# Block 0's start in another order: gates ahead of half the value's weights, one key weight tile on GpSimd, four constants behind the value's mixes, and block 1's statistics in two parts

## The chip, the cores and the metric

The kernel runs on one core of a Trainium2 chip. Its engines are TensorE (PE in the profile), VectorE (DVE), ScalarE (ACT), GpSimd (POOL) and SyncE (SP, which issues transfers). The metric is the device time of one execution in microseconds, the median of several; less is better.

## What is computed

One layer of an RWKV-like model over 2048 tokens of 512 features, in float32: a layer norm, an attention-like part with mixes of each token with its predecessor, a channel part, and a gated feed-forward part. Cut to what matters here, with `x` of the shape (1, 2048, 512):

```python
h = _layer_norm(x, ln1_g, ln1_b)
hh = _time_shift(h)
k = (h * tm_mk + hh * (1 - tm_mk)) @ Wk.T
v = (h * tm_mv + hh * (1 - tm_mv)) @ Wv.T
r = (h * tm_mr + hh * (1 - tm_mr)) @ Wr.T
wkv = _wkv_run(k, v, tm_first, tm_decay)   # elementwise: exponentials of k, and v
x = x + jax.nn.sigmoid(r) * wkv @ Wo.T
...                                          # channel part, then gated feed-forward part
```

## The kernel before

The tokens are cut into four blocks of 512. Activations lie with the features in the partitions, as four tiles of 128x512. A float32 product is made as three passes of TensorE: each operand is split into a high part (rounded, by a copy on ScalarE) and a low part (what the rounding left, by a subtraction on GpSimd or VectorE), and the passes are high x high, high x low and low x high (`three_passes`).

No scheduler orders the work. Each engine has its own program, written by hand, and the engines meet at counting semaphores. The order at the start of each program is what the change edits. For block 0 it goes so:

- The block's tokens are normed and transposed by TensorE into four PSUM banks. For each of r, k and v, ScalarE makes the previous token's share of a tile (`rest_of`, L746, into `made`), VectorE adds the token's own share (`mix`, L1123 and L1125; semaphore `op_made`), ScalarE makes the high part (`operand_hi`, L736; `op_hi`), and GpSimd the low part (`operand_lo`, L1459; `op_lo`). `made` is a ring of four tiles.
- Each weight matrix comes as four tiles. ScalarE makes the high parts (`matrix_hi`, L731; `w_hi`), and GpSimd (L1447) or VectorE (L1150, `matrix_lo`; for the last tile of Wr L1143) the low parts (`item_lo`).
- TensorE runs `receptance(0)` tile by tile as operands come (L517 to L521), then `key(0)` and `value(0)` bank by bank (`three_passes`, L485 to L487). A bank of `key(0)` is free when ScalarE's sigmoid has read the receptance from it (`receptance_gate`, L763; `r_gate`). A bank of `value(0)` is free when `wkv_weight` has read the key from it.
- `wkv_weight(0)` is shared by ScalarE (L770 into the bank, L773 into `e2`, L775 into the bank; it needs the constant `minus_bonus` and waits for `const_done` 7) and VectorE (L1160 for gate times `e2`, L1163 for bank times gate; `g_done`). `last_token` (twelve times L1107) saves the block's last token for the next block.
- In the middle of `value(0)` TensorE transposes block 1, which VectorE must have normed (`norm1(1)`) after its statistics (`norm1_stats(1)`: four bn_stats L1076, four bn_aggr L1079, L1050 and L1051) and after a power on GpSimd (`norm1(1)`, L1471).
- `later_constants` makes `minus_bonus` and the three constants of the channel part (L1041, L1035, L1036, L1038), each 128x4 or 128x8.

SyncE loads in one queue, in this order: block 0, the twelve tiles of Wr, Wk and Wv, block 1, Wo, and blocks 2 and 3. It isn't touched.

Of the kernel before, what the change touches and what calls it, by code (L numbers as in the profile page):

```python
# [30 lines left out]
KT = H // P  # L31
# [175 lines left out]
def build(nc, x, wts, wide, tall, vectors, identity, out):  # L207
# [3 lines left out]
    with ExitStack() as ctx:  # L211
# [117 lines left out]
        item_lo = [sem(f"item_lo{n}") for n in range(ITEMS // KT)]  # L329
        last_r_lo = sem("last_r_lo")  # L330
        const_done, table_loaded = sem("const_done"), sem("table_loaded")
# [150 lines left out]
        def _(pe):  # L482
# [18 lines left out]
            def features(kind, b, item, row, banks, done, bank_free, by_operand, halfway=None):  # L501
# [23 lines left out]
                else:  # L525
                    for j in range(KT):
                        if halfway is not None and j == KT // 2:
                            halfway()
                        bank_free(j)
                        for k in range(KT):  # L530
                            if j == 0:
                                if b == 0:
                                    pe.wait_ge(item_lo[item // KT], k + 1)
                                pe.wait_ge(op_lo, operand_at(kind, b) + k + 1)
                            mm = three_passes(banks[j][:], lambda p: weight(j, k, p),
                                              lambda p: place(kind, b, k, p), k == 0, k == KT - 1)
                        mm.then_inc(done, 1)
# [189 lines left out]
        def _(act):  # L727
# [249 lines left out]
            mixed("k", 0)  # L977
            matrix_hi(ITEM_V)
            receptance_gate(0)
            mixed("v", 0)  # L980
            act.wait_ge(const_done, 7)
# [45 lines left out]
        def _(dve):  # L1027
# [44 lines left out]

            def norm_stats(n, tile_of, stats, again=False):

                for s in range(SUBS):
                    dve.bn_stats(moments[:, s, :], tile_of(s)).then_inc(ln_moments, 1)  # L1076
                for s in range(SUBS):
                    dve.wait_ge(ln_moments, SUBS * n + s + 1)
                    dve.bn_aggr(stats[:, s, :], moments[:, s, :]).then_inc(ln_stats, 1)  # L1079
                dve.wait_ge(ln_stats, SUBS * (n + 1))  # L1080
                if again:
                    var_of_both(stats[:, :, 1], slice(None), ln_var)
                else:
                    dve.tensor_scalar(var_eps[:, 0], stats[:, :, 1], EPS, None, ALU.add).then_inc(ln_var, 1)

            def norm1_stats(b):
                dve.wait_ge(x_loaded[b - 1], 16)
                if b == BLOCKS - 1:
                    dve.wait_ge(ln_rstd, 3)
                norm_stats(nth_norm(1, b), lambda s: resid[:, b, s, :], stats1[:, b], again=True)  # L1090

# [286 lines left out]
            mix("r", 0)  # L1378
            later_constants()
            matrix_lo(ITEM_K, range(2))  # L1380
            mix("k", 0)
            matrix_lo(ITEM_K, range(2, KT))
            norm1_stats(1)
            mix("v", 0)
            last_token(0, 0)
            wkv_weight(0, range(2))
# [55 lines left out]
        def _(pool):  # L1442
            def matrix_lo(item, rows=range(KT)):
                for k in rows:
                    row = (item + k) % ROWS
                    pool.wait_ge(w_hi, item + k + 1)
                    pool.tensor_tensor(weights[:, row, 1, :], landing(item + k), weights[:, row, 0, :].bitcast(F32),  # L1447
                                       ALU.subtract).then_inc(item_lo[item // KT], 1)

            def x_added(b):  # L1450
# [84 lines left out]
            first_norm1()  # L1535
            pool.wait_ge(z1_ready, SUBS)
            matrix_lo(ITEM_R, range(KT - 1))
            operand_lo("r", 0)
            operand_lo("k", 0)
            matrix_lo(ITEM_V, range(3))  # L1540
            norm1(1)
            matrix_lo(ITEM_V, range(3, KT))
            operand_lo("v", 0)
            operand_lo("r", 1)
# [68 lines left out]
```

## Time and profile before

| | |
|---|---|
| time, median of 3 runs | 1074.23 us (1073.85 to 1074.23) |
| the profiled execution's own time | 1074.51 us |
| its span, first to last instruction | 1072.7 us |
| TensorE busy | 1057.1 us (99%), 4748 matmuls |
| VectorE, ScalarE, GpSimd busy | 632.5, 484.2 and 540.2 us |
| mean granted clock of TensorE | 0.998 |

Busy times are those of one profiled execution. Matmuls are pipelined, so a row's length is more than the distance to the next one: of two rows 0.227 us apart each is shown as 0.39 us. Instructions on the other engines overlap at their ends too. A line number is that of the kernel before, unless something else is said; in the changed kernel the lines stand 4 to 20 further down.

### The profile page before, as it was taken

The numbers are of one execution on the slowest core, as the hardware profiler recorded it, in microseconds if no ns is written. First come the engines' busy times: TensorE is split into PE (matmuls) and PEld (weight loads), VectorE is DVE, ScalarE is ACT, GpSimd is POOL, SyncE is SP. The second block draws the span as 40 slices with busy tenths as digits, with TensorE's granted clock in tenths as the row PEclk, the third lists the DMA queues.
The fourth block names the chain that finished last, engine by engine and source line by source line (L and its number), as shares of the span: only waits on it lengthen the run. The fifth ranks groups of instructions, "written<-read, shape, count | busy, mean of one in ns | idle before, by whom it ended". The sixth has DMA issues, their size and how long they took to land.

```text
span 1072.7 us, 13182 instructions
## 1 busy us (share of the span) xinstructions
PE 1057.1 (99%) x4748; PEld 873.8 (81%) x4748; DVE 632.5 (59%) x1104; ACT 484.2 (45%) x808; POOL 540.2 (50%) x453
## 2 busy tenths in 40 slices
PE   7999999999999999999999999999999999999998
PEld 6888888788888888888887888888887888888887
DVE  7888656786545545555459567676658333333334
ACT  6866676766444454333355433434354222222221
POOL 6686373735755545445345655555553333333322
PEclk9999999999999999999999999999999999999999
DMA  8002042267653345742412757564554464344422
GB/s 317 1 1 40 1 99 83 95 202 282 231 182 122 128 157 158 225 128 89 157 50 99 243 208 238 207 188 153 197 183 150 149 234 155 106 141 152 153 79 79
DMA packets 45234, 157.19 MB, mean 147 GB/s; under 512 B 4080, under 2 KB 4208, under 8 KB 40560
## 3 DMA queue, kind: packets, MB, share of 16 engines
q1 hardware_dynamic: 29712, 108.02, 28.8%
q0 software_dynamic: 15168, 48.24, 15.0%
q8 instruction: 38, 0.62, 0.2%
q14 instruction: 28, 0.23, 0.1%
q10 hardware_dynamic: 288, 0.09, 0.0%
HBM read 97.60 MB, written 58.72 MB: 146 GB/s over the span
## 4 chain that ended last, share of the span: by engine, by line
PE 87%; DVE 7%; POOL 2%; ACT 1%; DMA 1%; issue 1%; SPq 0%; ACTq 0%; DVEq 0%
PE bank L485 15%; PE bank L486 15%; PE bank L487 15%; PE bank L496 13%; PE bank L497 13%; PE bank L498 13%; DVE combo L1238 2%; DMA quart<-wide 1%; POOL operand L1459 1%; PE bank L555 1%; PE bank L653 1%; DVE resid L1264 1%; POOL weights L1447 0%; POOL weights L1459 0%; DVE raw L1245 0%
## 5 line engine op out<-in xcount | busy, mean ns | idle before, releaser
L1264 DVE TENSOR_TENSOR resid<-bank,resid 128x512 f32<-128x512 f32 x240 | 165.1, 690 | 239.8 <-PE bank L487 238.5
L1503 POOL TENSOR_TENSOR inner<-made,inner 128x512 fp32r<-128x512 f32 x128 | 166.8, 1326 | 200.5 <-ACT inner L871 200.5
L496 PE MATMUL bank<-combo,left 128*128 128x512 f32 x672 | 262.7, 391 | 4.7 <-DVE combo L1238 3.1
L498 PE MATMUL bank<-combo,left 128*128 128x512 f32 x672 | 261.5, 389 | 0.0
L497 PE MATMUL bank<-combo,left 128*128 128x512 f32 x672 | 261.5, 389 | 0.0
L485 PE MATMUL bank<-right,inner 128*128 128x512 f32 x512 | 199.2, 389 | 0.0
L486 PE MATMUL bank<-right,inner 128*128 128x512 f32 x512 | 199.2, 389 | 0.0
L487 PE MATMUL bank<-right,inner 128*128 128x512 f32 x512 | 199.2, 389 | 0.0
L1481 POOL TENSOR_TENSOR left<-quart,left 128x512 fp32r<-128x512 f32 x96 | 115.4, 1225 | 91.3 <-ACT left L839 46.8
L496 PEld LDWEIGHTS bank<-combo,left 128*128 128x128 f32 x672 | 126.1, 188 | 34.1 <-DVE combo L1238 4.0
L498 PEld LDWEIGHTS bank<-combo,left 128*128 128x128 f32 x672 | 126.1, 188 | 26.2
L497 PEld LDWEIGHTS bank<-combo,left 128*128 128x128 f32 x672 | 126.2, 188 | 25.7
L485 PEld LDWEIGHTS bank<-right,inner 128*128 128x128 f32 x512 | 96.1, 188 | 20.1
L487 PEld LDWEIGHTS bank<-right,inner 128*128 128x128 f32 x512 | 96.1, 188 | 20.0
L486 PEld LDWEIGHTS bank<-right,inner 128*128 128x128 f32 x512 | 96.1, 188 | 19.9
L1498 POOL TENSOR_TENSOR right<-tall_staged,right 128x512 fp32r<-128x512 f32 x62 | 80.8, 1312 | 59.2 <-ACT right L849 59.2
L892 ACT ACTIVATE made<-bank 128x512 f32<-128x512 f32 x64 | 38.1, 595 | 154.0 <-PE bank L498 154.0
L1459 POOL TENSOR_TENSOR operand<-made,operand 128x512 fp32r<-128x512 f32 x64 | 83.6, 1406 | 35.1 <-ACT operand L736 35.1
L1329 DVE TENSOR_TENSOR made<-bank,made 128x512 f32<-128x512 f32 x64 | 44.2, 691 | 60.4 <-ACT made L892 39.1
L871 ACT ACTIVATE inner<-made 128x512 fp32r<-128x512 f32 x128 | 77.2, 628 | 2.5 <-DVE made L1329 0.2
L880 ACT ACTIVATE made<-bank 128x512 f32<-128x512 f32 x64 | 37.6, 587 | 85.7 <-PE bank L498 85.7
L485 PE MATMUL bank<-operand,weights 128*128 128x512 f32 x176 | 69.5, 395 | 1.8 <-ACT held L763 1.8
(133 smaller groups left out, 1457.7 us busy)
## 6 DMA issues: line engine op xcount, KB each, us to landing
kept_left<-left SPq DMA_DIRECT2D x24, 1792.0 KB, 8.1
left<-kept_left POOLq DMA_DIRECT2D x24, 1024.0 KB, 6.9
left<-kept_left POOLq DMA_DIRECT2D x24, 768.0 KB, 5.0
tall_staged<-tall SPq DMA_DIRECT2D x64, 256.0 KB, 2.9
quart<-wide SPq DMA_DIRECT2D x24, 512.0 KB, 4.2
raw<-kept SPq DMA_DIRECT2D x32, 256.0 KB, 6.3
landed<-wts SPq DMA_DIRECT2D x20, 256.0 KB, 6.3
resid<-x POOLq DMA_DIRECT2D x4, 1024.0 KB, 9.2
```

Source lines behind the costliest of these rows:

```text
L485: pe.matmul(acc, left(0), right(0), start=first, stop=False)
L486: pe.matmul(acc, left(0), right(1), start=False, stop=False)
L487: return pe.matmul(acc, left(1), right(0), start=False, stop=last)
L496: pe.matmul(acc[:], hi, combo[:, c, k, 0, :], start=fresh and k == 0, stop=False, skip_group_check=True)
L497: pe.matmul(acc[:], hi, combo[:, c, k, 1, :], start=False, stop=False, skip_group_check=True)
L498: mm = pe.matmul(acc[:], lo, combo[:, c, k, 0, :], start=False, stop=k == 1, skip_group_check=True)
L871: act.activation(inner[:, h % 4, i, 0, :], made_at(n), ACT.Copy).then_inc(inner_hi, 1)
L1264: dve.tensor_tensor(tile, A[s][:], tile, ALU.add).then_inc(added, 1)
L1459: pool.tensor_tensor(place(kind, b, k, 1), made[:, (n + k) % RING, :], place(kind, b, k, 0).bitcast(F32), ALU.subtract).then_inc(op_lo, 1)
L1481: lo = pool.tensor_tensor(left[u % 2][:, 1, a[0]:a[0] + n, :], quart[:, a[0] + 1:a[0] + 1 + n, :], left[u % 2][:, 0, a[0]:a[0] + n, :].bit ...
L1498: pool.tensor_tensor(right[:, g % 2, i, 1, :], tall_staged[i][:], right[:, g % 2, i, 0, :].bitcast(F32), ALU.subtract).then_inc(right_lo, 1)
L1503: pool.tensor_tensor(inner[:, h % 4, i, 1, :], made_at(n), inner[:, h % 4, i, 0, :].bitcast(F32), ALU.subtract).then_inc(inner_lo, 1)
```

## The change

Five edits, all in block 0's start:

- On GpSimd, the first weight tile waits for `const_done` 3 in place of `z1_ready` 4. A new function `second_of_k_lo` makes the low part of Wk's tile 1 between the operands of r and of k, with a semaphore of its own, and TensorE's `key(0)` waits for that. Wv's fourth tile and the low operands of v now come ahead of `norm1(1)`.
- On ScalarE, `receptance_gate(0)` stands behind two of the four tiles of Wv in place of all four.
- On VectorE, `later_constants` is moved from ahead of k's mixes to behind v's mixes, and before k's mixes only tile 0 of Wk is left of two.
- On VectorE, `norm1_stats(1)` is cut in two: the four bn_stats stay ahead of v's mixes, and the rest stands behind the constants.

```diff
--- before.py
+++ after.py
@@ -327,7 +327,7 @@
         gate_kept = [sem(f"gate_kept{b}") for b in range(BLOCKS)]
         w_hi = sem("w_hi")
         item_lo = [sem(f"item_lo{n}") for n in range(ITEMS // KT)]
-        last_r_lo = sem("last_r_lo")
+        last_r_lo, second_k_lo = sem("last_r_lo"), sem("second_k_lo")
         const_done, table_loaded = sem("const_done"), sem("table_loaded")
         ln_moments, ln_stats, ln_var = sem("ln_moments"), sem("ln_stats"), sem("ln_var")
         ln_rstd, half_set = sem("ln_rstd"), sem("half_set")
@@ -529,8 +529,12 @@
                         bank_free(j)
                         for k in range(KT):
                             if j == 0:
-                                if b == 0:
+                                if b == 0 and kind != "k":
                                     pe.wait_ge(item_lo[item // KT], k + 1)
+                                elif b == 0 and k == 1:
+                                    pe.wait_ge(second_k_lo, 1)
+                                elif b == 0:
+                                    pe.wait_ge(item_lo[item // KT], max(k, 1))
                                 pe.wait_ge(op_lo, operand_at(kind, b) + k + 1)
                             mm = three_passes(banks[j][:], lambda p: weight(j, k, p),
                                               lambda p: place(kind, b, k, p), k == 0, k == KT - 1)
@@ -975,8 +979,9 @@
             mixed("r", 0, behind=1)
             matrix_hi(ITEM_K, range(1, KT))
             mixed("k", 0)
-            matrix_hi(ITEM_V)
+            matrix_hi(ITEM_V, range(2))
             receptance_gate(0)
+            matrix_hi(ITEM_V, range(2, KT))
             mixed("v", 0)
             act.wait_ge(const_done, 7)
             wkv_weight(0)
@@ -1070,10 +1075,14 @@
                     normed(s)
                 shares(slice(0, 3), 0)
 
-            def norm_stats(n, tile_of, stats, again=False):
-
+            def norm_moments(tile_of):
                 for s in range(SUBS):
                     dve.bn_stats(moments[:, s, :], tile_of(s)).then_inc(ln_moments, 1)
+
+            def norm_stats(n, tile_of, stats, again=False, moments_there=False):
+
+                if not moments_there:
+                    norm_moments(tile_of)
                 for s in range(SUBS):
                     dve.wait_ge(ln_moments, SUBS * n + s + 1)
                     dve.bn_aggr(stats[:, s, :], moments[:, s, :]).then_inc(ln_stats, 1)
@@ -1083,11 +1092,15 @@
                 else:
                     dve.tensor_scalar(var_eps[:, 0], stats[:, :, 1], EPS, None, ALU.add).then_inc(ln_var, 1)
 
-            def norm1_stats(b):
+            def norm1_moments(b):
+                dve.wait_ge(x_loaded[b - 1], 16)
+                norm_moments(lambda s: resid[:, b, s, :])
+
+            def norm1_stats(b, moments_there=False):
                 dve.wait_ge(x_loaded[b - 1], 16)
                 if b == BLOCKS - 1:
                     dve.wait_ge(ln_rstd, 3)
-                norm_stats(nth_norm(1, b), lambda s: resid[:, b, s, :], stats1[:, b], again=True)
+                norm_stats(nth_norm(1, b), lambda s: resid[:, b, s, :], stats1[:, b], True, moments_there)
 
             def norm1_tile(b, s):
                 dve.tensor_scalar(resid[:, b, s, :], resid[:, b, s, :], stats1[:, b, s, 0:1],
@@ -1376,12 +1389,13 @@
             last_of_r_lo()
             dve.wait_ge(const_done, 3)
             mix("r", 0)
-            later_constants()
-            matrix_lo(ITEM_K, range(2))
+            matrix_lo(ITEM_K, range(1))
             mix("k", 0)
             matrix_lo(ITEM_K, range(2, KT))
-            norm1_stats(1)
+            norm1_moments(1)
             mix("v", 0)
+            later_constants()
+            norm1_stats(1, moments_there=True)
             last_token(0, 0)
             wkv_weight(0, range(2))
             norm1(1)
@@ -1447,6 +1461,12 @@
                     pool.tensor_tensor(weights[:, row, 1, :], landing(item + k), weights[:, row, 0, :].bitcast(F32),
                                        ALU.subtract).then_inc(item_lo[item // KT], 1)
 
+            def second_of_k_lo():
+                row = ITEM_K + 1
+                pool.wait_ge(w_hi, row + 1)
+                pool.tensor_tensor(weights[:, row, 1, :], landing(row), weights[:, row, 0, :].bitcast(F32),
+                                   ALU.subtract).then_inc(second_k_lo, 1)
+
             def x_added(b):
 
                 pool.wait_ge(z2_ready, SUBS * (b + 1))
@@ -1533,14 +1553,14 @@
             pool.memset(minus_half[:], -0.5).then_inc(half_set, 1)
             pool.wait_ge(half_set, 1)
             first_norm1()
-            pool.wait_ge(z1_ready, SUBS)
+            pool.wait_ge(const_done, 3)
             matrix_lo(ITEM_R, range(KT - 1))
             operand_lo("r", 0)
+            second_of_k_lo()
             operand_lo("k", 0)
-            matrix_lo(ITEM_V, range(3))
+            matrix_lo(ITEM_V)
+            operand_lo("v", 0)
             norm1(1)
-            matrix_lo(ITEM_V, range(3, KT))
-            operand_lo("v", 0)
             operand_lo("r", 1)
             matrix_lo(ITEM_O)
             for b in range(1, BLOCKS):
```

VectorE, from the last mix of r to the first of k; before:

```order
L1125 SCALAR_TENSOR_TENSOR made<-bank,whole_g,whole_b 128x1
L1041 TENSOR_SCALAR minus_bonus<-vec 128x4
L1035 TENSOR_TENSOR whole_g<-vec 128x8
L1036 TENSOR_TENSOR whole_b<-vec 128x8
L1038 TENSOR_TENSOR rest_g<-vec,whole_g 128x8
L1150 TENSOR_TENSOR weights<-landed,weights 128x512 x2
L1123 SCALAR_TENSOR_TENSOR made<-bank,whole_g,made 128x511
L1125 SCALAR_TENSOR_TENSOR made<-bank,whole_g,whole_b 128x1
```

and now (L1136 and L1138 are the mixes, L1163 is the weight tile):

```order
L1138 SCALAR_TENSOR_TENSOR made<-bank,whole_g,whole_b 128x1
L1163 TENSOR_TENSOR weights<-landed,weights 128x512
L1136 SCALAR_TENSOR_TENSOR made<-bank,whole_g,made 128x511
L1138 SCALAR_TENSOR_TENSOR made<-bank,whole_g,whole_b 128x1
L1136 SCALAR_TENSOR_TENSOR made<-bank,whole_g,made 128x511
L1138 SCALAR_TENSOR_TENSOR made<-bank,whole_g,whole_b 128x1
L1136 SCALAR_TENSOR_TENSOR made<-bank,whole_g,made 128x511
L1138 SCALAR_TENSOR_TENSOR made<-bank,whole_g,whole_b 128x1
```

The four constants and one weight tile no longer stand between the mixes of r and those of k.

VectorE, from v's last mix to the first instruction of `wkv_weight` (L1160 of before, L1173 now); before:

```order
L1123 SCALAR_TENSOR_TENSOR made<-bank,whole_g,made 128x511
L1125 SCALAR_TENSOR_TENSOR made<-bank,whole_g,whole_b 128x1
L1107 SCALAR_TENSOR_TENSOR edge<-bank,rest_g,vec 128x1 x12
L1160 TENSOR_TENSOR held<-held,e_56 128x512
L1163 TENSOR_TENSOR held<-bank,held 128x512
```

and now:

```order
L1136 SCALAR_TENSOR_TENSOR made<-bank,whole_g,made 128x511
L1138 SCALAR_TENSOR_TENSOR made<-bank,whole_g,whole_b 128x1
L1046 TENSOR_SCALAR minus_bonus<-vec 128x4
L1040 TENSOR_TENSOR whole_g<-vec 128x8
L1041 TENSOR_TENSOR whole_b<-vec 128x8
L1043 TENSOR_TENSOR rest_g<-vec,whole_g 128x8
L1088 BN_AGGR stats<-moments 128x2 x4
L1055 TENSOR_SCALAR var_eps<-stats 128x4
L1056 TENSOR_SCALAR var_eps<-stats 128x4
L1120 SCALAR_TENSOR_TENSOR edge<-bank,rest_g,vec 128x1 x12
L1173 TENSOR_TENSOR held<-held,e_56 128x512
L1176 TENSOR_TENSOR held<-bank,held 128x512
```

The constants (L1046 to L1043) and the second half of block 1's statistics (L1088 to L1056) have come in ahead of `last_token` (L1120) and `wkv_weight`.

GpSimd, from the tiles of Wr to Wo; before (L1447 is a weight tile, L1459 a low operand, L1471 the power for block 1's norm):

```order
L1447 TENSOR_TENSOR weights<-landed,weights 128x512 x3
L1459 TENSOR_TENSOR operand<-made,operand 128x512 x8
L1447 TENSOR_TENSOR weights<-landed,weights 128x512 x3
L1471 TENSOR_TENSOR rstd<-var_eps,minus_half 128x8
L1447 TENSOR_TENSOR weights<-landed,weights 128x512
L1459 TENSOR_TENSOR operand<-made,operand 128x512 x8
L1447 TENSOR_TENSOR weights<-landed,weights 128x512 x4
```

and now (L1461 and L1467 are weight tiles, L1479 is a low operand, L1491 the power):

```order
L1461 TENSOR_TENSOR weights<-landed,weights 128x512 x3
L1479 TENSOR_TENSOR operand<-made,operand 128x512 x4
L1467 TENSOR_TENSOR weights<-landed,weights 128x512
L1479 TENSOR_TENSOR operand<-made,operand 128x512 x4
L1461 TENSOR_TENSOR weights<-landed,weights 128x512 x4
L1479 TENSOR_TENSOR operand<-made,operand 128x512 x4
L1491 TENSOR_TENSOR rstd<-var_eps,minus_half 128x8
L1479 TENSOR_TENSOR operand<-made,operand 128x512 x4
L1461 TENSOR_TENSOR weights<-landed,weights 128x512 x4
```

A weight tile now stands between the operands of r and of k, and the power stands behind the four operands of v.

## Rows read from the trace of the kernel before

**Rows 1.** The page: span, busy time and share of TensorE.

```profile
span 1072.7 us, 13182 instructions
...
PE 1057.1 (99%) x4748; PEld 873.8 (81%) x4748; DVE 632.5 (59%) x1104; ACT 484.2 (45%) x808; POOL 540.2 (50%) x453
```

**Rows 2.** Timeline of TensorE: start, length, instruction, idle time before it.

```profile
24.18 1.07 PE L521 MATMUL bank<-operand,weights 128*128 128x512 f32 x4
27.07 0.50 PE L485 MATMUL bank<-operand,weights 128*128 128x512 f32 x1 [1.82 <-ACT held L763]
...
28.43 0.63 PE L487 MATMUL bank<-operand,weights 128*128 128x512 f32 x1
...
39.68 0.39 PE L485 MATMUL bank<-operand,weights 128*128 128x512 f32 x1
```

**Rows 3.** Windows: stretch, length, busy time by engine, granted clock (PEclk), DMA share.

```profile
24.00:28.20 4.20, 2.38 (x11) 1.66 (x10) 4.20 (x5) 4.20 (x9) 4.20 (x4) 1.00 0.11 41
28.20:31.60 3.40, 3.40 (x10) 2.62 (x9) 3.37 (x11) 2.37 (x5) 3.40 (x3) 0.50 0.00 0
```

**Rows 4.** Timeline of ScalarE, columns as in rows 2.

```profile
17.31 1.66 ACT L731 ACTIVATE weights<-landed 128x512 fp32r<-128x512 f32 x3
...
21.48 0.63 ACT L736 ACTIVATE operand<-made 128x512 fp32r<-128x512 f32 x1 [0.51 <-DVE made L1125]
...
24.37 2.17 ACT L731 ACTIVATE weights<-landed 128x512 fp32r<-128x512 f32 x4
26.45 2.03 ACT L763 ACTIVATE held<-bank 128x512 f32<-128x512 f32 x4
...
34.41 0.64 ACT L770 ACTIVATE bank<-bank,minus_bonus 128x512 f32<-128x512 f32 x1
35.07 1.28 ACT L773 ACT_TABLE_LOAD   x1
36.37 0.60 ACT L773 ACTIVATE e<-bank 128x512 f32<-128x512 f32 x1
```

**Rows 5.** Timeline of VectorE.

```profile
17.01 1.26 DVE L1036 TENSOR_TENSOR whole_b<-vec 128x8 f32<-128x8 f32 x1
18.19 0.15 DVE L1038 TENSOR_TENSOR rest_g<-vec,whole_g 128x8 f32<-128x8 f32 x1
...
20.58 0.74 DVE L1123 SCALAR_TENSOR_TENSOR made<-bank,whole_g,made 128x511 f32<-128x511 f32 x1
...
23.72 3.25 DVE L1150 TENSOR_TENSOR weights<-landed,weights 128x512 fp32r<-128x512 f32 x2
26.89 2.46 DVE L1076 BATCH_NORM_STATS2 moments<-resid 128x6 f32<-128x512 f32 x4
...
29.66 0.97 DVE L1050 TENSOR_SCALAR var_eps<-stats 128x4 f32<-128x4 f32 x1
...
33.76 1.59 DVE L1107 SCALAR_TENSOR_TENSOR edge<-bank,rest_g,vec 128x1 f32<-128x1 f32 x12
...
37.79 0.69 DVE L1163 TENSOR_TENSOR held<-bank,held 128x512 f32<-128x512 f32 x1
```

**Rows 6.** Timeline of GpSimd.

```profile
14.44 5.07 POOL L1459 TENSOR_TENSOR operand<-made,operand 128x512 fp32r<-128x512 f32 x4
22.19 5.94 POOL L1459 TENSOR_TENSOR operand<-made,operand 128x512 fp32r<-128x512 f32 x4 [2.68 <-ACT operand L736]
28.09 3.77 POOL L1447 TENSOR_TENSOR weights<-landed,weights 128x512 fp32r<-128x512 f32 x3
31.81 1.64 POOL L1471 TENSOR_TENSOR rstd<-var_eps,minus_half 128x8 f32<-128x8 f32 x1
```

**Rows 7.** VectorE's L1051 after block 0 (durations in ns), and L1160 in block 0.

```profile
L1051 DVE TENSOR_SCALAR var_eps<-stats x3: 157/157/1332, 30.6 to 103.1; 128x4 f32<-128x4 f32 x3
...
L1160 DVE TENSOR_TENSOR held<-held,e x4: 685/693/1829, 37.1 to 44.7; 128x512 f32<-128x512 f32 x4
```

**Rows 8.** Timeline of TensorE near 827.

```profile
827.17 0.50 PE L496 MATMUL bank<-combo,left 128*128 128x512 f32 x1 [1.95 <-DVE combo L1238]
```


## The prediction, made before the changed kernel ran

> **What bounds the kernel now.** I first read the page: TensorE is busy for 1057.1 of 1072.7 us [rows 1]. Only its gaps and its slow stretches can be won, unless work is taken from it, and this change takes none. Then I read TensorE's timeline around the edited code [rows 2]. The receptance of block 0 ends with four matmuls from 24.18; the last starts near 24.86 and the next could start 0.23 later, at 25.1. The key of block 0 starts at 27.07, after an idle time of 1.82 us that the row puts down to ScalarE's sigmoid, `receptance_gate(0)`. From 28.4 at the latest the matmuls take 0.63 us apiece instead of 0.39. The windows say why: the granted clock is 1.00 up to 28.2 and 0.50 from 28.2 to 31.6 [rows 3], that is 1.2 GHz in place of 2.4. TensorE fell 1.1 us after it had started again, and 3.4 us at half speed cost 1.7 us. So the place has lost 1.8 + 1.7 = 3.5 us, 0.33% of the time. That is all a perfect edit could give here.
>
> Then I read ScalarE, VectorE and GpSimd over the same stretch [rows 4 to 6], to see what is late next.
>
> **The lock that sets the sizes.** Small VectorE operations sometimes take over a microsecond: the 128x8 product of L1036 takes 1.26 us and the one after it, L1038, only 0.15; L1050 takes 0.97 on 128x4 elements; two weight tiles of L1150 take 3.25 where L1160 does a tile of that size in 0.69 at best [rows 5, 7]. Each long one ends where a GpSimd tile ends (18.20, 30.6). Mixes, products from PSUM and bn_stats beside the same GpSimd tiles keep their length. So a VectorE operation that reads two SBUF tensors, or a tensor_scalar in SBUF, waits for the end of GpSimd's running tile and holds back the next one by some 0.45 us: four tiles of `operand_lo("k")` fill 22.19 to 28.09, or 5.9 us, against 3.72 us for three undisturbed (28.09 to 31.81, so 1.24 each) [rows 6]. After a wait of this kind a second small operation mostly slips through; one in three L1051 did not and took 1332 ns [rows 7].
>
> The Trainium skill (SBUF — State Buffer, "Who interferes with whom") has the same rule: whoever starts first holds the pair of ports that VectorE and GpSimd share for its whole instruction. By that rule the small operations are not free beside a busy GpSimd; without it the sum below would come out 2.2 us lower. The trace agrees, with the 1.26 and the 0.15 us.
>
> **The change, part by part.**
>
> *GpSimd's first wait.* `const_done` 3 comes three small products of VectorE, at most 0.15 us each [rows 5], after the last norm tile that it waited for. GpSimd's first tiles start up to 0.3 us later. What this moves is the low operands of r, which TensorE takes up in turn with its own work: I take nothing, and hold 0.3 us as the bound.
>
> *Constants away from the key, one key tile to GpSimd.* Between the mixes of r and of k, VectorE now does one tile in place of four constants and two tiles. It is ready for k's mixes near 17.9 instead of 20.58, but ScalarE's share of the first (L746) isn't done before 19.5 (three K tiles from 17.31, 0.52 each, and 0.76), so the mixes start about 19.6, 1.0 us sooner. ScalarE's first operand_hi of k still stands behind three L746 and comes at 20.8 instead of 21.48. ScalarE is free at 23.6 instead of 24.37 [rows 4]. GpSimd's added tile (1.24) lies in the pause that it had before 22.19, from 20.2 to 21.4, and the k tiles start at 21.45. With two of them held back by VectorE's tiles 2 and 3, as before, they end at 27.3.
>
> *Gates ahead of half the V tiles.* ScalarE does two V tiles (1.04) to 24.65, and the gates when the bank is done: receptance's first bank ends its row near 24.6, so the gate starts at 24.75 and ends at 25.3 (0.57) instead of 27.02. `key(0)` starts at 25.35, 1.7 us sooner. It wants its four low operands at 25.4, 26.1, 26.8 and 27.5; they come at 22.7, 24.0, 25.7 and 27.3. All fit, the last by 0.1 to 0.2 us. No gap worth a fall of the clock is left, so 48 matmuls at 0.227 us end at 36.35 instead of 39.68 [rows 2]. Up to here 3.3 us are won. The V tiles' loads stand ahead of block 1's in SP's in-order queue; no step here issues or moves a transfer.
>
> *What is late next: `value(0)`.* Its first bank waits for `g_done` 1 (L1163), which needs ScalarE's exponentials, and they need `const_done` 7. I follow GpSimd's tile ends, since VectorE's small operations now meet them. GpSimd is busy without a pause from 21.45: k to 27.3, V to 32.25 (4 x 1.24), v to 37.25 (tile ends 33.5, 34.75, 36.0), and only then `norm1(1)`, 1.60 long. VectorE: tile 3 of K ends near 26.2, bn_stats 2.4 more, mixes of v from 28.6 (0.79 each, the last held by ScalarE to 30.95), free at 31.75. There L1041 waits for 32.25 and L1036 for 33.5, so `const_done` 7 is at 33.65. Four bn_aggr (0.35) lead to L1050, which waits for 34.75; then the twelve L1107 (1.5) end at 36.35. ScalarE, free at 32.4, waits to 33.7; L770 0.66, table load 1.29, exp 0.60: e2 at 36.3 [rows 4]. L1160 thus arrives at 36.35, inside the tile that ends at 37.25, then takes 0.6, and L1163 0.69: `g_done` 1 at 38.6, against 37.79 + 0.69 = 38.48 before [rows 5]. The constants and the statistics have moved from before the key to before the value's gate, and that gate isn't sooner at all.
>
> So `value(0)` starts at 38.65 instead of 39.68: 1.0 us sooner, with a new gap of 38.65 - 36.35 = 2.3 us. This is longer than the 1.82 after which the clock fell. The other long gap in the trace, 1.95 us before 827.17 [rows 8], was followed by no fall, so a gap near two microseconds may go either way; 2.3 us more likely falls. A fall costs 1.7 us again (1.6 if it starts inside the gap). The second bank is wanted at 41.4 or later; L1160 and L1163 for it end at about 40.6, behind the 1.60 of `norm1(1)`. The tiles of `norm1(1)` end at 42.4, wanted at 44.1. Nothing else is late.
>
> **Sum.** -1.0 for the earlier start and +1.6 for the clock over the same stretch are +0.6 us. The profiled execution took 1074.51, of which 1.81 lie outside its span; it stands 0.28 above the median 1074.23. 1074.51 + 0.6 - 0.28 gives 1074.8. Of the work behind value(0) everything follows TensorE and moves with it.
>
> **The rivals.**
> 1. *The same gap without the fall* (0.20): -1.0, 1073.2. For it stands the gap of 1.95 us; against it the fall after 1.82. The Trainium skill (TensorE: Matmul & The Clock Gate, "Part 1") says that the point of the change varies with where the matmuls lie in time; no row here shows that.
> 2. *The four constants slip between two tiles* (0.14), as pairs of them do [rows 5]. Then `const_done` 7 is at 32.5, L1160 meets the end at 36.0, `g_done` 1 is at 37.35 and the gap is 1.0. The second bank (40.6) then holds TensorE 0.5. That is -1.8 to -2.3: 1072.2 on average. If a stretch of the lock is also missed behind it, the full 3.3: 1070.9 (0.04).
> 3. *Slower: one more tile of waiting* (0.20). If L1035, L1038 or L1051 is caught like the 1332 ns one, all is 1.24 later; L1160 then arrives behind 37.25, finds GpSimd in `norm1(1)` until 38.85, and `g_done` 1 is at 40.2. The value starts 0.6 us later than before, with a gap of 3.9 us, and the fall adds up to 1.7, since part of it lies in the gap: +0.6 to +2.3, mean 1075.8. It decides from the point at which L1160 arrives after 37.25.
> 4. The change does what it says and nothing waits for it: this is rival 2's end, 1070.9, held in its 0.04.
>
> **Numbers.** The forecast has 0.42, within 0.5 us of 1074.8 by the bounds of my sums. What this kernel's timing can tell from no change is about 0.2%, 2.15 us: under 1072.1 or over 1076.4. Faster takes half of rival 2 with its 0.04, and some of rival 1 where small errors add (0.13); slower takes rival 3's upper part (0.12); the rest, 0.75, is no change. The range runs from 1072.3 to 1076.8, from rival 2's better half to just over rival 3's upper end.
>
> **What would show it.** In the new profile: the gate's wait before `key(0)` under 0.4 us and no fall at 28; `key(0)` over near 36.4; GpSimd without a pause from 21.5 to 38.9; long small operations among the constants near 32 and 33; a TensorE wait of about 2.3 us put down to VectorE's L1163 just before 38.7, and granted clock 0.50 for 3.4 us about there. Wrong would be: low operands of k later than TensorE (a second gap near 27), a value start before 37.5, or a clock of 1.00 through 42.

## The result, and the profile after

| | changed kernel | kernel before |
|---|---|---|
| median of 9 runs | 1076.97 us (1076.62 to 1078.62) | 1074.23 us (1073.78 to 1075.91) |
| ratio, 95% interval | 1.0024 [1.0014, 1.0033] | |
| profiled execution | 1077.34 us, span 1075.5 us | 1074.51 us, span 1072.7 us |

The change makes the kernel 2.7 us slower, and the interval of the ratio lies wholly above 1. The forecast of 1074.8 us is missed, and the time lies 0.2 us past the range's upper end of 1076.8 us. One execution among the experiments below (of e2) took 1521.8 us at a mean granted clock of 0.656, and the ratios leave it out. The page of the changed kernel:

```profile
span 1075.5 us, 13182 instructions
...
PE 1058.7 (98%) x4748; PEld 874.8 (81%) x4748; DVE 631.6 (59%) x1103; ACT 484.3 (45%) x808; POOL 541.2 (50%) x454
```

TensorE is busy 1.6 us longer than in [rows 1] with the same 4748 matmuls, and the span is 2.8 us longer. TensorE's timeline of the changed kernel, against [rows 2]:

```profile
24.16 1.07 PE L521 MATMUL bank<-operand,weights 128*128 128x512 f32 x4
25.24 0.50 PE L485 MATMUL bank<-operand,weights 128*128 128x512 f32 x1
...
36.19 0.39 PE L487 MATMUL bank<-operand,weights 128*128 128x512 f32 x1
40.30 0.50 PE L485 MATMUL bank<-operand,weights 128*128 128x512 f32 x1 [3.72 <-DVE held L1176]
...
40.91 0.63 PE L487 MATMUL bank<-operand,weights 128*128 128x512 f32 x1
```

The gap ahead of `key(0)` is gone, and the last matmul of the key starts at 36.19. Then TensorE stands still until 40.30, waiting for `g_done` 1 (L1176 is the L1163 of before), and from 40.91 its matmuls take 0.63 us. The windows of the changed kernel show the same in the granted clock, against [rows 3]:

```profile
24.00:28.20 4.20, 4.19 (x18) 2.97 (x17) 4.20 (x6) 4.19 (x9) 4.20 (x3) 1.00 0.14 50
28.20:31.60 3.40, 3.40 (x16) 2.79 (x15) 3.38 (x9) 3.40 (x7) 3.40 (x4) 1.00 0.00 0
...
36.20:40.30 4.10, 0.38 (x2) 0.00 (x1) 3.98 (x20) 4.00 (x6) 2.76 (x2) 1.00 0.01 2
...
40.90:44.30 3.40, 3.40 (x10) 2.65 (x9) 3.37 (x7) 2.57 (x5) 0.00 (x0) 0.51 0.00 0
```

The stretch at 0.50 has moved from behind the key's start to behind the value's. Who holds `g_done` 1 is read backwards from 40.30. VectorE's timeline of the changed kernel, against [rows 5]:

```profile
31.59 0.21 DVE L1138 SCALAR_TENSOR_TENSOR made<-bank,whole_g,whole_b 128x1 f32<-128x1 f32 x1
31.71 0.67 DVE L1046 TENSOR_SCALAR minus_bonus<-vec 128x4 f32<-128x4 f32 x1
32.30 1.33 DVE L1040 TENSOR_TENSOR whole_g<-vec 128x8 f32<-128x8 f32 x1
33.55 1.32 DVE L1041 TENSOR_TENSOR whole_b<-vec 128x8 f32<-128x8 f32 x1
34.80 1.32 DVE L1043 TENSOR_TENSOR rest_g<-vec,whole_g 128x8 f32<-128x8 f32 x1
36.15 0.38 DVE L1088 BATCH_NORM_AGGREGATE stats<-moments 128x2 f32<-128x6 f32 x4
36.57 0.78 DVE L1055 TENSOR_SCALAR var_eps<-stats 128x4 f32<-128x4 f32 x1
37.26 0.16 DVE L1056 TENSOR_SCALAR var_eps<-stats 128x4 f32<-128x4 f32 x1
37.33 1.59 DVE L1120 SCALAR_TENSOR_TENSOR edge<-bank,rest_g,vec 128x1 f32<-128x1 f32 x12
38.84 0.68 DVE L1173 TENSOR_TENSOR held<-held,e 128x512 f32<-128x512 f32 x1
39.55 0.69 DVE L1176 TENSOR_TENSOR held<-bank,held 128x512 f32<-128x512 f32 x1
```

The four constants take from 31.71 to 36.12. Three products of 128x8 elements, of which one took 0.15 us in [rows 5], take 1.33, 1.32 and 1.32 us one right behind the other. GpSimd's timeline of the changed kernel, against [rows 6], has the same rhythm:

```profile
21.37 5.96 POOL L1479 TENSOR_TENSOR operand<-made,operand 128x512 fp32r<-128x512 f32 x4
27.28 5.07 POOL L1461 TENSOR_TENSOR weights<-landed,weights 128x512 fp32r<-128x512 f32 x4
32.31 5.01 POOL L1479 TENSOR_TENSOR operand<-made,operand 128x512 fp32r<-128x512 f32 x4
37.50 1.64 POOL L1491 TENSOR_TENSOR rstd<-var_eps,minus_half 128x8 f32<-128x8 f32 x1 [0.18 <-DVE var_eps L1056]
```

Four tiles in 5.01 us are 1.25 us each, the distance between the starts of the products. ScalarE's timeline of the changed kernel, against [rows 4], shows who stands behind the constants:

```profile
36.15 0.66 ACT L774 ACTIVATE bank<-bank,minus_bonus 128x512 f32<-128x512 f32 x1 [3.69 <-DVE rest_g L1043]
36.83 1.28 ACT L777 ACT_TABLE_LOAD   x1
38.12 0.60 ACT L777 ACTIVATE e<-bank 128x512 f32<-128x512 f32 x1
```

ScalarE is idle for 3.69 us until the last constant, L1043. Its clamp, table load and exponential end at 38.7. VectorE's own row also stands behind the last constant: the statistics (L1088 to L1056) and the twelve L1120, which end at 38.9. So two chains lead from 36.1 to L1173, and they end 0.2 us apart. L1173 and L1176 end at 40.24, and 0.06 later the value starts. In the kernel before, ScalarE started its exponential at 36.37 [rows 4]. By my comparison of the two traces, the value starts 0.62 us later than before, the transposes of block 1 in the middle of it 2.4 us later, from 279 us on all is 2.7 us later, and the end 2.8.

### The profile page after: what moved, and what is told of

The parts are those of the page before. It is cut to its first block, busy times and chain, and to the rows that moved or that the text cites. A ratio compares the mean times of both kernels' runs of the same rounds, so it can differ in the third digit from the quotient of the medians.

```text
span 1075.5 us, 13182 instructions
## 1 busy us (share of the span) xinstructions
PE 1058.7 (98%) x4748; PEld 874.8 (81%) x4748; DVE 631.6 (59%) x1103; ACT 484.3 (45%) x808; POOL 541.2 (50%) x454
## 4 chain that ended last, share of the span: by engine, by line
PE 88%; DVE 7%; POOL 2%; ACT 1%; issue 1%; DMA 0%; ACTq 0%; DVEq 0%
PE bank L485 15%; PE bank L487 15%; PE bank L486 15%; PE bank L496 14%; PE bank L498 13%; PE bank L497 13%; DVE combo L1251 2%; POOL weights L1461 1%; POOL operand L1479 1%; PE bank L559 1%; PE bank L657 1%; DVE resid L1277 1%; POOL weights L1479 0%; DVE made L1136 0%; DVE moments L1080 0%
## 5 line engine op out<-in xcount | busy, mean ns | idle before, releaser
L1479 POOL TENSOR_TENSOR operand<-made,operand 128x512 fp32r<-128x512 f32 x64 | 83.5, 1404 | 35.9 <-ACT operand L740 35.9
```

The lines of the kernel that those rows point to most:

```text
L1479: pool.tensor_tensor(place(kind, b, k, 1), made[:, (n + k) % RING, :], place(kind, b, k, 0).bitcast(F32), ALU.subtract).then_inc(op_lo, 1)
```

## The experiments

Theory (C in the expectations): each small constant waits for the end of one whole GpSimd tile, ScalarE waits for all four, and so the value waits. Rivals: something else of the change costs the time (the sooner gates, the split statistics, the moved key tile), or the place of the constants as such. Where an expectation gives a letter to a theory, the text beside it says what it holds. Diffs are against the changed kernel unless another is named; "before beside" is the kernel before, timed on the same chip.

**e1_constants_back**: the constants between the mixes of r and Wk's tile 0.

```diff
             mix("r", 0)
+            later_constants()
             matrix_lo(ITEM_K, range(1))
...
             mix("v", 0)
-            later_constants()
```

> The changed kernel with one part undone: the four constants stand again between r's mixes and VectorE's tile 0 of Wk. Theory C (the constants behind v's mixes each wait for the end of a GpSimd tile, 1.33 us apiece in the changed kernel's rows, and hold ScalarE's exponentials from 32.5 to 36.15): value(0) starts near 37.4 instead of 40.30, the idle time before it is about 1.0 us, the clock does not fall, and the time is 1.5 to 2.5 us under the kernel before (about 1072.2). Theory G (GpSimd's chain of tiles and its power for block 1 set the value's gate, whatever VectorE does): value(0) starts at 39 or later and the time stays at 1076 to 1077.

Measured: 1074.08 us, before beside 1074.58, ratio 0.9996 [0.9988, 1.0005]. `value(0)` starts at 37.66, behind an idle time of 0.83 us. The place of the constants alone was worth 2.6 us of value start and, by the ratios (0.9996 against 1.0024), all of the loss. The time missed the expected gain of 1.5 to 2.5 us over the kernel before: it isn't clear of no change. The profiled execution (1072.85) was the fastest of the 11, and what the others lost stands in no trace.

**e2_three_late**: only `minus_bonus` behind v's mixes, the three that the last tokens of later mixes need behind `wkv_weight(0)`; ScalarE waits for `const_done` 4. Run again as **e2b_three_late**, for a trace at full clock.

```diff
-            act.wait_ge(const_done, 7)
+            act.wait_ge(const_done, 4)
             wkv_weight(0)
...
-            later_constants()
+            bonus_constant()
             norm1_stats(1, moments_there=True)
             last_token(0, 0)
             wkv_weight(0, range(2))
+            channel_constants()
```

> The changed kernel with one thing moved: the three constants of the channel part (128x8 each) stand behind wkv_weight(0), where GpSimd is idle, and ScalarE waits for minus_bonus alone (const_done 4). Theory C: the three small products cost three GpSimd tile ends where they stood; here each takes 0.15 to 0.2 us, ScalarE's L774 starts at 32.5 instead of 36.15, value(0) starts between 37.4 (if the statistics' second small operation slips through) and 38.7, and the time is 1.0 to 2.3 us under the kernel before. Theory G: value(0) starts at 39 or later, time 1076 to 1077. Rival S (it is the statistics cut in two that delay last_token and the gate): little gain, 1075 to 1076.

> The same kernel as the one with three constants late, for a trace at full clock. Theory C: L774 starts at 32.5, three operations of 0.16 us after 43 where GpSimd is idle, value(0) between 37.4 and 38.7, span 1071.0 to 1072.2 without a fall of the clock and 1.1 to 1.7 more with one.

Measured: 1075.10 us and 1075.28, before beside 1074.58 and 1074.89, ratios 1.0002 [0.9993, 1.0011] and 1.0001 [0.9992, 1.0011]. Neither median shows the gain of 1.0 to 2.3 us that was expected. Without GpSimd beside them the three products take 0.16, 0.16 and 0.17 us (e2b, VectorE; the first of them):

```profile
44.65 0.16 DVE L1041 TENSOR_TENSOR whole_g<-vec 128x8 f32<-128x8 f32 x1
```

The value starts at 38.67, at the late end of what was expected: the statistics' two tensor_scalars now meet GpSimd's tiles (0.93 and 1.33 us) and L1176 (the L1173 of the changed kernel) takes 1.57. So a part of the wait moved to the next small operations in the row. ScalarE's exponential is done at 35.06 and the last tokens only at 36.4, so here VectorE's own row holds the value, not ScalarE.

**e3_gates_alone**: the kernel before, with only the gates ahead of half the value's weights.

```diff
-            matrix_hi(ITEM_V)
+            matrix_hi(ITEM_V, range(2))
             receptance_gate(0)
+            matrix_hi(ITEM_V, range(2, KT))
```

> The kernel before with one part of the change alone: the gates ahead of half of Wv's tiles. key(0) starts near 26.1 instead of 27.07 with an idle time under 1.0 us, the clock does not fall at 28, and key(0) is over near 37. The value's gate stays where it was (38.48), so value(0) starts at 38.55 with an idle time of 1.4 us. Without a fall of the clock there the time is 1.1 us under the kernel before (1073.1); with one it is 0.5 us over it (1074.8).

Measured: 1074.94 us, before beside 1074.58, ratio 1.0004 [0.9996, 1.0013]. TensorE's two starts in e3:

```profile
26.00 0.50 PE L485 MATMUL bank<-operand,weights 128*128 128x512 f32 x1 [1.07 <-ACT held L763]
...
38.53 0.50 PE L485 MATMUL bank<-operand,weights 128*128 128x512 f32 x1 [1.19 <-DVE held L1164]
```

The key starts 1.07 us sooner and no clock fell, yet the value starts only 1.15 us sooner than at 39.68 [rows 2]: it stands at its gate. So the gate of the value, which I had put at 38.48 for the kernel before, takes back most of what the key wins. Of the 3.5 us at most 1.15 could be won while that gate stood where it was. The median shows not even that: the profiled execution (1073.73) was the fastest of the 12, and six of the others show a fall of the clock.

**e4_constants_alone**: the kernel before, with only the constants moved behind v's mixes.

> The kernel before with one part of the change alone: the four constants behind v's mixes. Theory C: they fall among GpSimd's tiles of v (34.65 to 40.16), each waits for a tile end, const_done 7 comes at 38 to 39, value(0) starts at 41.5 to 43 instead of 39.68, and the time is 2 to 5 us over the kernel before. If the small operations slip through in pairs as in the trace of before, it is 1 us less. Theory G: no change to 0.5 us.

Measured: 1077.21 us, before beside 1074.58, ratio 1.0024 [1.0015, 1.0034], as large a loss as the changed kernel's from one line that is moved, with the statistics whole and GpSimd in its old order. It lies inside the expected 2 to 5 us. In the profiled execution of e4 the constants went in two pairs (0.98, 0.15, 1.25, 0.15 us), from 32.92, since all of block 1's statistics stand ahead of them, and the value started at 40.17. That execution (1075.08, no fall of the clock) was the fastest of the 11, so no trace shows how the median of 1077.21 came about.

**e5_bonus_early**, and again as **e5b_bonus_early**: as e2, but `minus_bonus` between r's mixes and Wk's tile 0.

> The changed kernel with the four constants taken apart: minus_bonus alone stands between r's mixes and VectorE's tile 0 of Wk, the other three behind wkv_weight(0), where GpSimd is idle; ScalarE waits for const_done 4. Theory C (small VectorE operations wait for GpSimd's tile ends): none of the four is on the way to the value's gate; ScalarE's L774 starts at 32.4 (36.15 in the changed kernel), value(0) starts near 37.6 as with the constants put back, and where the clock does not fall the span is 1071.0 to 1072.2, as there. If the place of the constants between r and k was itself worth something, key(0) starts up to 0.4 us sooner than the 25.47 of that run, but the value's gate does not move with it. Theory G (GpSimd's chain sets the gate): 39 or later, which the run with the constants put back already speaks against.

> The kernel with minus_bonus early and the other three constants late once more, beside the changed kernel on one chip. Theory C: 2.5 to 4 us under the changed kernel and 0.5 to 1.5 us under the kernel before, value(0) near 37.3.

Measured: 1074.20 us and 1072.97, before beside 1074.89 and 1074.83, ratios 0.9989 [0.9981, 0.9998] and 0.9987 [0.9977, 0.9996]. This version beats both kernels, by about 1.3 us the one before (by the two ratios). Against e10, the changed kernel on the same chip, e5b is 6.4 us faster, more than the expected 2.5 to 4, since e10 itself came out slow. TensorE in e5b:

```profile
37.09 0.50 PE L485 MATMUL bank<-operand,weights 128*128 128x512 f32 x1 [0.83 <-DVE held L1179]
```

**e6_one_more**: the changed kernel with one more 128x8 product among the constants (its output is read by nobody).

```diff
+        spare = sb("spare", [P, 2, KT])
...
+                dve.tensor_tensor(spare[:], vec[:, 8:10, :], beta, ALU.mult)
```

> The changed kernel with one more 128x8 product of two SBUF tensors (into a tile that nobody reads) among the constants behind v's mixes. Its own work is 0.16 us. Theory C: it is caught by a GpSimd tile like the three beside it, takes 1.3 us, const_done 7 comes at 37.3 instead of 36.12, and value(0) starts 0.8 to 1.2 us later than 40.30; the time rises by as much. If the lock did not matter, 0.1 us.

Measured: 1078.42 us, before beside 1074.89, ratio 1.0034 [1.0021, 1.0048]. The products take 1.32, 1.32, 1.32 and 1.30 us, the clamp of ScalarE starts at 37.05 instead of 36.15, and the value at 41.19 instead of 40.30. A product of 0.15 us costs 0.9 us of start. The two ratios differ by 0.0010, or 1.1 us, but that isn't clear of noise: their intervals overlap, and the changed kernel alone came out at 1.0024 here and at 1.0032 in e10.

**e7_gates_behind**, and the same kernel as **e12_gates_behind** and **e13_gates_behind**: the gates back behind all four V tiles.

> The changed kernel with the gates put back behind all four tiles of Wv. Theory C: key(0) starts near 26.1 instead of 25.24, but what it loses is only idle time taken from in front of value(0), which still starts at 40.3; the time stays within 0.3 us of the changed kernel, that is 1.8 to 3 us over the kernel before, and TensorE's clock falls once as there. If the early key is worth anything in this kernel, the time rises by 0.8 us.

> The changed kernel with its gates back behind all four value tiles, as in e7_gates_behind, looked at again. If the same code has both outcomes: here or in e13 the four constants take under 3 us in all, in pairs of about 1.3 and 0.16, and value(0) starts before 39. If the code decides: all four take about 1.33 us each again, with value(0) near 39.9 in both looks.

> The same kernel as e12_gates_behind, the second look: both outcomes possible if chance within one code decides (a run near 1072 to 1073.5 has the pairs), about 1.33 us for each constant again if the code decides.

Measured: e7 1076.69 us (10 runs, 1073.6 to 1079.55), before beside 1074.89, ratio 1.0014 [1.0003, 1.0024], or 1.5 us over the kernel before, just under the expected 1.8 to 3; e12 1074.91 and e13 1075.31, one run each, before beside 1074.91. The same code has more than one outcome. In e7's profiled execution all four constants waited (1.24, 1.33, 1.32, 1.32 us). In e12's they went in pairs:

```profile
31.29 0.23 DVE L1045 TENSOR_SCALAR minus_bonus<-vec 128x4 f32<-128x4 f32 x1
31.43 0.15 DVE L1039 TENSOR_TENSOR whole_g<-vec 128x8 f32<-128x8 f32 x1
31.51 1.26 DVE L1040 TENSOR_TENSOR whole_b<-vec 128x8 f32<-128x8 f32 x1
32.70 0.15 DVE L1042 TENSOR_TENSOR rest_g<-vec,whole_g 128x8 f32<-128x8 f32 x1
```

and in e13's the products waited one by one:

```profile
30.61 0.19 DVE L1045 TENSOR_SCALAR minus_bonus<-vec 128x4 f32<-128x4 f32 x1
30.72 1.34 DVE L1039 TENSOR_TENSOR whole_g<-vec 128x8 f32<-128x8 f32 x1
31.98 1.33 DVE L1040 TENSOR_TENSOR whole_b<-vec 128x8 f32<-128x8 f32 x1
33.23 1.32 DVE L1042 TENSOR_TENSOR rest_g<-vec,whole_g 128x8 f32<-128x8 f32 x1
...
35.72 1.32 DVE L1055 TENSOR_SCALAR var_eps<-stats 128x4 f32<-128x4 f32 x1
```

The value started at 37.82 in e12 and at 39.91 in e13: 2.1 us between two executions of one kernel. The constants ended 1.7 us later in e13, and the statistics' second small operation (L1055) waited too, where it took 0.15 in e12. The exponential was done at 37.16 and the last tokens at 38.5, so VectorE's own row held the value in e13. So chance within one code is shown. The two times are only 0.4 us apart, since the clock fell once in e12, near 826 us, and not at all in e13. It is no even chance, though: every one of the 14 runs of the changed kernel, here and in e10, took 1076.6 us or more.

**e8_stats_whole**: the statistics of block 1 whole again, ahead of v's mixes; the constants stay behind.

```diff
-            norm1_moments(1)
+            norm1_stats(1)
             mix("v", 0)
             later_constants()
-            norm1_stats(1, moments_there=True)
```

> The changed kernel with the split of block 1's statistics undone: all of norm1_stats(1) ahead of v's mixes, the constants still behind them. Theory C: the statistics' two small operations are now caught ahead of the mixes (1 to 2 tile ends), the mixes of v end 1.3 to 2.6 us later than 31.7, the constants are caught as before and const_done 7 comes about 1.2 us later than 36.12; value(0) starts near 41.3 instead of 40.30, and the time is 0.7 to 1.3 us over the changed kernel's. Rival S (the split itself is what costs): value(0) starts sooner than 40.30 and the time falls by 1 us or more.

Measured: 1075.27 us, before beside 1074.83, ratio 1.0007 [0.9998, 1.0017]. My theory had said 0.7 to 1.3 us over the changed kernel; it came out 1.8 us under it by the ratios, which is the side of rival S (the split itself is what costs). VectorE in e8:

```profile
31.61 0.54 DVE L1046 TENSOR_SCALAR minus_bonus<-vec 128x4 f32<-128x4 f32 x1
32.06 0.15 DVE L1040 TENSOR_TENSOR whole_g<-vec 128x8 f32<-128x8 f32 x1
32.13 1.26 DVE L1041 TENSOR_TENSOR whole_b<-vec 128x8 f32<-128x8 f32 x1
33.31 0.15 DVE L1043 TENSOR_TENSOR rest_g<-vec,whole_g 128x8 f32<-128x8 f32 x1
```

This is what I had assumed for the changed kernel: two waits, the last constant written at 33.5, the value at 38.43 (I had put it at 38.65). So the loss was there with the constants behind v's mixes and the statistics whole (e4), and with the same two things here it isn't clear of noise. The split isn't needed for the loss, but it isn't cleared of a share in it: whether it costs something as such, or only changes the moment at which the constants meet GpSimd, is not shown.

**e9_key_tile_back** (tile 1 of Wk back on VectorE) and **e10_as_changed** (the changed kernel as it is, for the same chip).

> The changed kernel with tile 1 of Wk back on VectorE. VectorE is ready for k's mixes at 17.6 and ScalarE's share comes at 19.4, so the tile fits between, even if a GpSimd tile catches it (1.2 us): key(0) starts at 25.2 to 25.4, value(0) at 40.3, time within 0.3 us of the changed kernel. If the hand-over was worth something, key(0) starts 0.5 us or more later, which by theory C still leaves the value's start and the time where they are.

> The changed kernel as it is, beside the other three on one chip, for a direct comparison: 1.9 to 3.1 us over the kernel before, one fall of the clock in each execution, by any theory.

Measured: e9 1077.84 us, ratio 1.0026 [1.0015, 1.0037]; e10 1079.35 us (5 runs), ratio 1.0032 [1.0019, 1.0045]; before beside 1074.83. All four constants wait in both, and the value starts at 40.57 and 40.13. The moved key tile is neither the cause of the loss nor a gain that could be seen. e10 came out slower than expected, 4.5 us over the kernel before and not 1.9 to 3.1, with a mean clock of 0.995 in three of its 5 executions. Of the change's five edits, GpSimd's new order was not undone by itself.

**e11_gpsimd_waits**: a wait is added to the changed kernel; GpSimd starts the low operands of v only when the constants are written.

```diff
             matrix_lo(ITEM_V)
+            pool.wait_ge(const_done, 7)
             operand_lo("v", 0)
```

> The changed kernel with one wait added: GpSimd starts the value's low tiles only when VectorE has written the last of the four constants. Nothing on VectorE or ScalarE moves. Theory (each constant waits for the end of one of GpSimd's tiles of about 1.33 us): the first constant still waits for the tile that runs, to about 32.3, and the four then run in about 0.7 us, since GpSimd stands still; the last is written near 33, not 36.1, ScalarE's clamp of block 1 starts there instead of at 36.15, and value(0) starts at 37.5 to 38.5 instead of 40.3, with GpSimd's tiles 0.7 us later, which nothing near it waits for. The time is 1.5 to 3 us under the changed kernel, that is 1074 to 1075.5, although a wait has been added. Rival (the four are late by their place behind the mixes, not by GpSimd): each still takes about 1.3 us or the last stands at 36 or later, now with GpSimd late by 4 us as well, and the time is 1077 or more.

Measured: 1073.14 us, before beside 1074.91, ratio 0.9985 [0.9976, 0.9995]; 3.8 us under the changed kernel's 1076.97, or 4.2 by the two ratios, which are taken on different chips. VectorE in e11:

```profile
31.75 0.55 DVE L1046 TENSOR_SCALAR minus_bonus<-vec 128x4 f32<-128x4 f32 x1
32.21 0.15 DVE L1040 TENSOR_TENSOR whole_g<-vec 128x8 f32<-128x8 f32 x1
32.29 0.15 DVE L1041 TENSOR_TENSOR whole_b<-vec 128x8 f32<-128x8 f32 x1
32.40 0.17 DVE L1043 TENSOR_TENSOR rest_g<-vec,whole_g 128x8 f32<-128x8 f32 x1
```

GpSimd and TensorE in e11:

```profile
32.65 5.48 POOL L1479 TENSOR_TENSOR operand<-made,operand 128x512 fp32r<-128x512 f32 x4 [0.38 <-DVE rest_g L1043]
```

```profile
37.77 0.50 PE L485 MATMUL bank<-operand,weights 128*128 128x512 f32 x1 [1.27 <-DVE held L1176]
```

The same four instructions in the same place end at 32.6 instead of 36.1, and GpSimd starts its tiles 0.34 us later for it and is through with them 0.8 us later (38.13 against 37.32), where TensorE doesn't wait for it. The value starts 2.5 us sooner. 8 of 10 runs showed no fall of the clock at all and took 1072.7 to 1073.7; the two with a fall took 1074.5, inside the expected 1074 to 1075.5. The rival, that the place as such costs the time, has fallen.

## Why the prediction was wrong

The step that failed is this sentence: "There L1041 waits for 32.25 and L1036 for 33.5, so `const_done` 7 is at 33.65." It took from [rows 5] that a second small operation slips through behind one that waited. All four waited, and `const_done` 7 stood at 36.12, 2.5 us late. The text had the counterexample (L1051 at 1332 ns) and gave it one more tile of about 1.25 us as rival 3; it was two, at a place where GpSimd has twelve tiles in a row.

By its other steps:

- *Key.* Right. Gate and key: `key(0)` at 25.24 (25.35 foreseen), no fall at 28, last matmul at 36.19 and over at 36.4 (36.35), k's low operands from 21.37 to 27.33 (21.45 to 27.3), v's mixes done at 31.7 (31.75).
- *Behind the constants.* Foreseen were the last tokens' end at 36.35 and `g_done` 1 at 38.6; they stood at 38.9 and 40.24. Of the 2.5 us, 0.8 came back: L1173 arrived when GpSimd had left its tiles and took 0.68 us, without the wait to 37.25 that I had counted. GpSimd was then in its power (L1491, 37.50 to 39.14), and L1173 did not wait for that.
- *Sum.* Start of the value: -1.0 foreseen, +0.62 measured. Clock: +1.6 foreseen, 1.75 measured (from +0.62 at the value's start to +2.37 at the transposes). That this term came right is in part luck: the fall stood behind a gap of 3.9 us, and behind gaps near the foreseen 2.3 (2.07 us in e2b, 2.08 in e8, 2.88 in e4) there was none. Behind it: 0 foreseen, +0.36 measured near 279 us, where one gap of TensorE is 0.62 us and not 0.25. It isn't the change's: e10, the same code, has 0.22 there, and e11 0.67. 0.62 + 1.75 + 0.36 = 2.7, against +0.6.
- *What the place had to give.* "That is all a perfect edit could give here", 3.5 us, was too much by two thirds, as long as the value's gate stood at my own number of 38.48: e3 shows 1.15 us. More is to be had only where that gate comes sooner too, as in e5b (37.09, 2.6 us sooner). So a fall of the clock ahead of a gate that binds anyway costs only what comes out past the gate. And not every execution had a fall: of the 98 runs of the kernel before that stood beside the experiments, 22 kept a full clock, with spans about 1.2 us shorter. Against that, all 9 runs of the changed kernel show one. Where it stood, only a trace tells: in the profiled executions of e5, e8 and e12 the one fall was near 826 us.
- *The lock's share.* That the sum "would come out 2.2 us lower" without the lock counts the start alone; with no gap the clock's 1.6 would go too, and the text's own rival 4 is 3.9 us lower.
- *Rivals.* Rival 3, at 0.20, had the lock and the side right, with a value start of 40.2 (40.30 measured) and a gap of 3.9 us (3.88 from 36.42). That these numbers fit so well is luck: it came to 40.2 by one more tile and a wait for GpSimd's power to 38.85, and measured were two more tiles and no wait for the power. Its price, +0.6 to +2.3, was too small by the 0.36 at 279 us and by taking a part of the fall off.

The Trainium skill (SBUF — State Buffer, "Who interferes with whom") calls the ports that VectorE shares with GpSimd an exclusive lock. e11 agrees, with 0.15 us for a product beside a standing GpSimd against 1.33 beside a running one.

What stays open: what decides whether a second small operation gets in behind the first. The starts in the traces do not tell the cases apart: L1040 starts at 32.06 and GpSimd's next row at 32.06 in e8, where it slips through, and at 32.30 and 32.31 in the changed kernel, where it waits. A kernel that keeps the two apart doesn't need the answer.

## What to carry to other kernels

Beside back-to-back GpSimd tiles, price each small tensor_tensor or tensor_scalar of VectorE that reads SBUF alone at up to one whole tile (1.25 us here; four bn_aggr kept their 0.38 us together, so it isn't every operation on SBUF), and keep what others wait for out of such a stretch: do it early, or let GpSimd stand still for it (0.8 us of GpSimd bought 3.8 us of time here). Before you count what a removed gap may give, look up when the next gate opens; what comes sooner than that is not won. Two places in the row of an engine are not of equal worth because the operations between them are small.

## What the runs showed of the hardware

- A fall of the clock is not decided by the length of the gap alone. After 3.54 us of idle time in e13 the clock stayed at 1.00, as the windows of e13 show (stretch, length, busy time by engine, granted clock, DMA share):

```profile
36.00:39.80 3.80, 0.38 (x2) 0.00 (x0) 3.77 (x15) 2.87 (x5) 2.65 (x2) 1.00 0.00 0
39.80:44.00 4.20, 4.08 (x18) 3.38 (x19) 4.07 (x9) 3.07 (x7) 0.00 (x0) 1.00 0.00 0
```

  After 3.72 us in the changed kernel, and after 1.82 us in the kernel before, it fell. The gap of [rows 8] tells the same more sharply: 16 traces have it near 826 us with 1.95 to 1.96 us, and the clock fell behind it in four (e5, e8, e10, e12) and stayed at 1.00 in the other twelve, the kernel before among them. In e8:

```profile
826.10:829.50 3.40, 3.40 (x9) 2.66 (x10) 1.75 (x3) 0.00 (x0) 0.00 (x0) 0.54 0.24 77
```

- The low clock can last twice as long. In e10 some 6.8 us at 0.50 go with a gap of 3.71 us, the first 0.6 of them still inside it (worked out from the two granted clocks below). Its execution took 1079.66 us against 1077.34 for the same code in the first profile, but the longer stretch isn't the whole difference, as the clock fell a second time, at 831 us. The first fall:

```profile
36.30:40.10 3.80, 0.13 (x1) 0.00 (x0) 3.71 (x17) 3.71 (x6) 2.50 (x2) 0.92 0.01 2
40.10:47.00 6.90, 6.87 (x18) 5.41 (x19) 5.89 (x10) 4.35 (x8) 0.00 (x0) 0.55 0.00 0
```

- Two executions of one kernel (e12, e13) differ by 2.1 us at one gate, by how the four constants and the second small operation of the statistics, of 0.15 to 0.2 us each, meet the tiles of GpSimd.
